# A Mamba layer stack on one core: the softplus correction moves from VectorE to GpSimd and ScalarE, and one product with C moves the other way

## The chip, the core and the metric

The kernel runs on one core of a Trainium2 chip. Its time is the device time of one launch in microseconds (us). Three runs of the kernel before took 16158.87, 16161.65 and 16184.59 us; their median is 16161.65 us.

## The reference

Sixteen sequences of 324 tokens (196 image patches and 128 text tokens) with 192 channels are embedded, normalized, and passed through sixteen Mamba layers; a mixture of sixteen experts follows. Nearly all of the time goes to the Mamba layers. For each layer, cut to what matters:

```python
h = rmsnorm(x, nw)
u, z = split(h @ in_w.T)                       # 2 x 384 channels
u = silu(causal_conv(u, cw, cb))               # 4 taps
dt_r, Bm, Cm = split(u @ xp_w.T)               # 48, 16, 16
dt = softplus(dt_r @ dtw.T + dtb)
A = -exp(a_log)
# scan over the 324 tokens, 384 channels x 16 states:
h = exp(dt * A) * h + (dt * u) * Bm
y = sum_n(h * Cm) + u * D
x = x + (y * silu(z)) @ ow.T
```

## The kernel before, in words

`run_layers` treats one layer of one sequence as a unit: 16 layers by 16 sequences are 256 units. Each engine runs its own endless program of steps, one step per unit, and the engines meet only at semaphores. A step `u` scans unit `u` and at the same time prepares the following ones: step-size work (softplus, z) for unit `p = u+1`, in-projection, convolution and x-projection for `k = u+2`, and the norm for `j = u+3`. The order of work on each engine is written out by hand: a step runs over `n = 0..15`, and each `n` holds one of sixteen scan passes and a few other pieces that are tied to that `n`.

One scan pass `s` covers 128 partitions by 972 elements (a quarter of the 16 states times 384 channels over 324 tokens). ScalarE writes `exp(dt*A)` into one of two PSUM buffers (`se_decay`, L602, three instructions), GpSimd writes `dtu*B` into one of four buffers (`ge_dbu`, L820), VectorE runs the scan into one of eight buffers `h` (`ve_scan`, L770). Then `h` is multiplied by C in place. VectorE does this from a PSUM copy of C that TensorE broadcasts once for four passes (`te_bcast` L439, `ve_product` L779). For the passes listed in `ON_POOL = (3, 7, 13)` GpSimd does it (`ge_product`, L828), from a copy `c_rep` in SBUF that a DMA has replicated. TensorE adds the products up, two passes at a time (`te_sum`, L452, eight matmul records). `SUM_AT` says at which `n` of the TensorE step each pair is added.

All small projections of TensorE share one PSUM bank `pj`, so they take strict turns with the ScalarE instruction that empties it: z in two halves (`te_z` L481, emptied by `se_z` L626), the output projection in two halves (`te_out` L496 and L498, emptied by `se_out` L632), u in two halves (`te_u` L516, `se_ur` L638), the convolution in two halves (`te_conv` L530, `se_conv` L645), the x-projection (`te_xp` L550), the step size in two halves (`te_dt` L559, emptied by `se_dt` L697/L698), and the sum of squares (`te_ss` L542).

The step size is `softplus(x) = relu(x) + log(1 + e)`, with `e = exp(-abs(x))`. The logarithm of a rounded `1 + e` loses digits of a small `e`, so the kernel corrects it. ScalarE computes `e` (`se_softplus` step 0, L704, at n = 0), `log(1 + e)` into `dtu` (step 1, L708, at n = 1), and the rounded `1 + e` into `u_pre` (step 2, L712, at n = 2, between the first z half and the decay of pass 3). VectorE then computes `(u_pre - 1) - dtu` into `dtu` in one instruction (`ve_log_error`, L794, after scan pass 3 and product 2). GpSimd builds `dt = dt + e` (L841, n = 4), `dt = dt - dtu` (L845, n = 8) and `dtu = dt * u` (L849, n = 8).

SyncE issues the DMAs in a fixed order, each behind the waits it needs. It stores `dt` and `dtu` to DRAM and loads them back replicated over partitions: four loads `dtu_rep` (`sp_load_dtu`, L914), each behind the GpSimd pass that last reads its buffer (12 to 15), and four loads `dt_rep` (`sp_load_dt`, L907), each behind the decay pass that last reads its buffer (12 to 15). All four `dtu_rep` loads and the last load of B stand ahead of the first `dt_rep` load. The next unit's decay pass 0 needs `dt_rep` 0.

Of the kernel before, what the change touches and what calls it, by code (L numbers as in the profile page):

```python
# [7 lines left out]
ALU = mybir.AluOpType  # L8
# [25 lines left out]
NR = 4  # L34
RING = 8
DRING = 4
ON_POOL = (3, 7, 13)
EPS = 1e-5
HALF_ULP = 2.0 ** -24

# [46 lines left out]
def embed(nc, cst, x_T, ins, raw_tables):  # L87
# [32 lines left out]
    with ExitStack() as ctx:  # L120
# [21 lines left out]
        with nc.Block() as block:  # L142
# [12 lines left out]
            @block.vector  # L155
            def _(dve):
                dve.memset(cst["eps"][:, :], EPS)
                dve.memset(cst["one"][:, :], 1.0)
                dve.memset(cst["ones96"][:, :], 1.0)
                dve.wait_ge(s_w, 32)  # L160
                done = 0
                for q in range(4):
                    hy, hx = q // 2, q % 2
                    oh, ow = (1 - hy), 2 * (1 - hx)
                    keep_h, keep_w = 1 - oh, 2 - ow
                    k_of = lambda a, b: w[:, 1 + a + b, 2 * q:2 * q + 2, :]
                    v = lambda i: wv[:, 2 * q:2 * q + 2, i, :]

                    for out, a, b in ((3, w[:, 0, 2 * q:2 * q + 2, :], k_of(keep_h, keep_w)),
                                      (1, v(3), k_of(keep_h, ow)),  # L170
                                      (2, v(3), k_of(oh, keep_w)),
                                      (0, v(1), k_of(oh, keep_w)),
                                      (0, v(0), k_of(oh, ow))):
                        wait(dve, s_v, done)
                        dve.tensor_tensor(v(out), a, b, ALU.add).then_inc(s_v, 1)
                        done += 1
# [129 lines left out]
def run_layers(nc, cst, x_T, params, weights, b_rows, dt_rows, dtu_rows):  # L306

    ident, ones96, sel_c, fold = cst["ident"], cst["ones96"], cst["sel_c"], cst["fold"]
    with ExitStack() as ctx:
# [74 lines left out]
        s_dtp = sem("s_dtp")  # L384
        s_dtev = sem("s_dtev")
        s_sp = sem("s_sp")
        s_d1 = sem("s_d1")
        s_dt = sem("s_dt")
        s_cq = sem("s_cq")
        s_z = sem("s_z")  # L390
# [170 lines left out]
            mm.then_inc(s_dtp, 1)  # L561


        SUM_AT = {3: 0, 6: 1, 7: 2, 10: 3, 11: 4, 13: 5}

        def tensor_step(pe, u, par, scan=True, a1=True, b1=True):

            p, k, j = u + 1, u + 2, u + 3
            for n in range(N):
                if scan and n % 4 == 1:  # L570
                    te_bcast(pe, u, par, n // 4)
                if n == 0:
                    te_ss(pe, j, b1)
                if n in (0, 1) and scan:
                    te_sum(pe, u, n - 2)
                if n in (1, 2) and b1:
                    te_z(pe, p, 1 - par, n - 1)
                if n in (3, 4) and scan:
                    te_out(pe, u, n - 3)
                if n in (5, 6) and a1:  # L580
                    te_u(pe, k, par, n - 5, scan, b1)
                if n in (8, 9) and a1:
                    te_conv(pe, k, n - 8)
                if n == 12 and a1:
                    te_xp(pe, k, par)
                if n in (13, 14) and a1:
                    te_dt(pe, k, n - 13)
                if scan and n in SUM_AT:
                    te_sum(pe, u, SUM_AT[n])
                if n == 7 and scan:  # L590
                    te_skip(pe, u, par, 0)
                    te_skip(pe, u, par, 1)
# [47 lines left out]
        def se_conv(act, k, half):  # L640
            reached(act, s_cv, 2 * k + half + 1)
            if half == 0:
                reached(act, s_ua, k)
                reached(act, s_d1, k)
            act.copy(half_of(u_pre, half), pj).then_inc(s_cvev, 1)  # L645

        def se_silu(act, k, par, b1):
# [43 lines left out]
        def se_dt(act, k, half):  # L691
            reached(act, s_dtp, 2 * k + half + 1)
            if half == 0:
                reached(act, s_sp, 3 * k)
                wait(act, s_dst[0], 16 * k)
                wait(act, s_dst[1], 16 * k)
            act.activation(half_of(exp_x, half), pj, ACT.Abs)  # L697
            act.activation(half_of(dt, half), pj, ACT.Relu).then_inc(s_dtev, 1)  # L698

        def se_softplus(act, p, step):  # L700
# [2 lines left out]
                reached(act, s_dtev, 2 * p + 2)  # L703
                act.activation(exp_x[:, :], exp_x[:, :], ACT.Exp, scale=-1.0).then_inc(s_sp, 1)  # L704
            elif step == 1:
                reached(act, s_sp, 3 * p + 1)
                wait(act, s_dst[1], 16 * p)
                act.activation(dtu[:, :], exp_x[:, :], ACT.Ln, bias=cst["one"][:, 0:1]).then_inc(s_sp, 1)  # L708
            else:
                reached(act, s_d1, p)  # L710
                reached(act, s_ua, p + 1)
                act.activation(u_pre[:, :], exp_x[:, :], ACT.Identity, bias=cst["one"][:, 0:1]).then_inc(s_sp, 1)  # L712

        def se_c_rows(act, p, par):
            reached(act, s_xpev, p + 1)
# [72 lines left out]
                              y_ps, z_act[par][:, :, :].rearrange("p i t -> p (i t)").rearrange("p (a b) -> p a b", a=2),  # L788
                              ALU.mult).then_inc(s_gate, 1)

        def ve_log_error(dve, p):

            reached(dve, s_sp, 3 * p + 3)
            dve.scalar_tensor_tensor(out=dtu[:, :], in0=u_pre[:, :], scalar=-1.0, in1=dtu[:, :],  # L794
                                     op0=ALU.add, op1=ALU.subtract).then_inc(s_d1, 1)

        def vector_step(dve, u, par, scan=True, a1=True, b1=True):
            p = u + 1
            other = 1 - par
            for n in range(N):  # L800
# [4 lines left out]
                if scan:  # L805
                    if n - 1 not in ON_POOL:
                        ve_product(dve, u, n - 1)
                if n == 3 and b1:
                    ve_log_error(dve, p)


        def ge_dbu(pool, u, s):
# [24 lines left out]
        def ge_dt(pool, p, par, step):  # L837

            if step == 0:
                reached(pool, s_sp, 3 * p + 1)  # L840
                pool.tensor_tensor(dt[:, :], dt[:, :], exp_x[:, :], ALU.add).then_inc(s_dt, 1)  # L841
            elif step == 1:
                reached(pool, s_dt, 3 * p + 1)
                reached(pool, s_d1, p + 1)
                pool.tensor_tensor(dt[:, :], dt[:, :], dtu[:, :], ALU.subtract).then_inc(s_dt, 1)  # L845
            else:
                reached(pool, s_dt, 3 * p + 2)
                reached(pool, s_ua, p + 1)
                pool.tensor_tensor(dtu[:, :], dt[:, :], u_act[par][:, :, :].rearrange("p i t -> p (i t)"), ALU.mult).then_inc(s_dt, 1)  # L849

        def gpsimd_step(pool, u, par, scan=True, a1=True, b1=True):
            p = u + 1
            for n in range(N):
                if scan:
                    ge_dbu(pool, u, n)
                    if (n - 4) % N in ON_POOL:
                        ge_product(pool, u if n >= 4 else u - 1, (n - 4) % N)
                if n == 4 and b1:
                    ge_dt(pool, p, 1 - par, 0)
                if n == 8 and b1:  # L860
                    ge_dt(pool, p, 1 - par, 1)
                    ge_dt(pool, p, 1 - par, 2)
                if n == 10:
                    ge_x_norm(pool, u + 3, 1 - par)

# [27 lines left out]

        def sp_store_dt(sp, p, which):

            reached(sp, s_dt, 3 * p + 2 + which)
            sp.sem_inc(s_go, 1)
            for s in (s_dur if which else s_dtr):
                wait(sp, s, 16 * p)
# [17 lines left out]
        def sync_step(sp, u, par, scan=True, a1=True, b1=True, reload=None):  # L917
# [9 lines left out]
                if reload and q < 2:  # L927
                    reload(q)
            if b1:
                for r in range(NR):  # L930
                    sp_load_dtu(sp, u, r)
                sp_load_b(sp, u, par, 3)
                for r in range(2):
                    sp_load_dt(sp, u, r)
            if reload:
                reload(2)
            if b1:
# [45 lines left out]
        with nc.Block() as block:  # L983
# [90 lines left out]

            @block.vector
            def _(dve):
                raise_counts(dve, s_scan, s_prod, s_gate, s_d1)
                for d in decay:
                    dve.memset(d, 0.0).then_inc(s_free, 1)
                for i in range(RING):  # L1080
# [670 lines left out]
def program(nc, ins, out):  # L1751
# [6 lines left out]
    with ExitStack() as ctx:  # L1758
        def sb(name, shape, dt=F32):
# [2 lines left out]
        cst = {  # L1762
            "ident": sb("ident", [128, 128]), "ones96": sb("ones96", [HC, HC]),
            "sel_c": sb("sel_c", [80, NQ, 128]), "fold": sb("fold", [128, 32]), "eps": sb("eps", [128, 1]),
            "one": sb("one", [128, 1]),
        }
        with ExitStack() as stream:
            x_T = stream.enter_context(nc.sbuf_tensor("x_T", [HC, 2, T], F32))
# [105 lines left out]
```

## Time and profile before

| what | us |
|---|---|
| median of three runs | 16161.65 |
| profiled execution, its own time | 16150.05 |
| its span in the trace | 16148.2 |
| VectorE busy | 13797.9 |
| TensorE busy (matmul) | 13519.5 |
| GpSimd busy | 13365.1 |
| ScalarE busy | 11298.1 |

The mean granted clock of TensorE over the span was 0.903.

The span is measured from the first to the last instruction; the own time is 1.85 us more. All rows below are from that one execution. A line number such as L770 is the line of the kernel file that issued an instruction; where no operand is named the row is about the queue itself. "Idle" in brackets is how long the engine sat idle ahead of a row and what it was released by. The granted clock (PEclk) is 1.00 where TensorE ran at 2.4 GHz and 0.50 where it ran at 1.2 GHz.

### The profile page before, as it was taken

The numbers are of one execution on the slowest core, as the hardware profiler recorded it, in microseconds if no ns is written. First come the engines' busy times: TensorE is split into PE (matmuls) and PEld (weight loads), VectorE is DVE, ScalarE is ACT, GpSimd is POOL, SyncE is SP. The second block draws the span as 40 slices with busy tenths as digits, with TensorE's granted clock in tenths as the row PEclk, the third lists the DMA queues.
The fourth block names the chain that finished last, engine by engine and source line by source line (L and its number), as shares of the span: only waits on it lengthen the run. The fifth ranks groups of instructions, "written<-read, shape, count | busy, mean of one in ns | idle before, by whom it ended". The sixth has DMA issues, their size and how long they took to land. (4 is left out here: it accounts for less than half of the span.)

```text
span 16148.2 us, 205785 instructions
## 1 busy us (share of the span) xinstructions
PE 13519.5 (84%) x52202; PEld 6684.0 (41%) x52202; DVE 13797.9 (85%) x9806; ACT 11298.1 (70%) x21632; POOL 13365.1 (83%) x6095
## 2 busy tenths in 40 slices
PE   6888888888888888888888888888888888887689
PEld 4334434433343343343434334444434433434367
DVE  2999999999999999999999999999999999993643
ACT  3777777777777777777777777777777777773111
POOL 1999999999999999999999999999999999990023
PEclk7989999999999999989999998888989999997799
DMA  2333333333333333333333333333333333331022
GB/s 71 114 118 110 112 122 108 115 112 120 108 116 119 112 111 118 114 110 124 108 115 111 121 109 113 118 114 111 109 123 108 115 115 117 110 119 32 9 52 58
DMA packets 714479, 1703.22 MB, mean 105 GB/s; under 512 B 89033, under 2 KB 369462, under 8 KB 714162
## 3 DMA queue, kind: packets, MB, share of 16 engines
q1 hardware_dynamic: 693666, 1685.54, 31.4%
q0 software_dynamic: 19968, 15.98, 0.6%
q14 instruction: 109, 0.89, 0.0%
q10 hardware_dynamic: 720, 0.55, 0.0%
q8 instruction: 16, 0.26, 0.0%
HBM read 1414.96 MB, written 286.74 MB: 105 GB/s over the span
## 5 line engine op out<-in xcount | busy, mean ns | idle before, releaser
L820 POOL TENSOR_TENSOR dbu<-dtu_rep,b_rep 128x972 f32<-128x972 f32 x4096 | 9131.1, 2250 | 1066.6 <-DVE h L770 1041.0
L770 DVE TENSOR_TENSOR_SCAN h<-ps,dbu 128x972 f32<-128x972 f32 x4096 | 8825.4, 2169 | 1050.6 <-ACT ps L602 1049.6
L602 ACT ACTIVATE ps<-dt_rep,A_cur 128x323 f32<-128x323 f32 x12288 | 5881.6, 521 | 987.0 <-DVE h L770 806.6
L452 PE MATMUL ps<-h,fold 128*32 128x486 f32 x16400 | 4149.9, 668 | 78.2 <-DVE h L779 77.1
L779 DVE TENSOR_TENSOR h<-h,ps 128x972 f32<-128x972 f32 x3329 | 3800.2, 1142 | 105.2 <-PE ps L439 102.4
L828 POOL TENSOR_TENSOR h<-h,c_rep 128x972 f32<-128x972 f32 x769 | 1964.0, 2554 | 2.2 <-DVE h L770 2.2
L452 PEld LDWEIGHTS ps<-h,fold 128*32 128x32 f32 x16400 | 854.7, 119 | 2453.0 <-issue 2002.0
L530 PE MATMUL ps<-u_raw,w_cv 128*128 128x162 f32 (+7 forms) x8256 | 1801.9, 371 | 2.8 <-ACT u_raw L638 1.5
L530 PEld LDWEIGHTS ps<-u_raw,w_cv 128*128 128x128 f32 x8256 | 1359.4, 190 | 458.4 <-ACT u_pre L645 115.7
L1632 POOL DMA_INDIRECT e_rows<-n_rows,e_ix x96 | 96.9, 1010 | 1306.0 <-issue 1213.8
L439 PE MATMUL ps<-c_rows,sel_c 16*128 16x324 f32 x2048 | 882.6, 512 | 332.6 <-DVE h L779 332.5
L516 PE MATMUL ps<-x_norm,w_u 96*128 96x324 f32 (+1 forms) x4128 | 987.4, 383 | 202.1 <-ACT u_raw L638 196.2
L481 PE MATMUL ps<-x_norm,w_z 96*128 96x324 f32 (+1 forms) x4112 | 1011.6, 390 | 168.9 <-ACT z_pre L626 168.2
L550 PE MATMUL ps<-u_act,w_x 128*128 128x324 f32 x1548 | 538.1, 488 | 575.1 <-ACT u_act L653 568.1
L498 PE MATMUL ps<-y_gated,w_o 128*96 128x324 f32 x3084 | 1008.4, 466 | 0.0
L481 PEld LDWEIGHTS ps<-x_norm,w_z 96*128 96x128 f32 x4112 | 677.6, 195 | 624.9 <-issue 273.5
L516 PEld LDWEIGHTS ps<-x_norm,w_u 96*128 96x128 f32 x4128 | 664.6, 190 | 517.6 <-ACT u_raw L638 259.8
L632 ACT COPY x_T<-ps 96x324 f32 (+1 forms) x514 | 218.2, 424 | 922.8 <-PE ps L498 922.8
L559 PE MATMUL ps<-xp_rows,w_dt 49*128 49x162 f32 (+1 forms) x2064 | 696.0, 467 | 169.3 <-ACT xp_rows L689 165.4
L645 ACT COPY u_pre<-ps 128x486 f32<-128x486 f32 x516 | 290.9, 564 | 673.9 <-PE ps L530 673.8
L439 PEld LDWEIGHTS ps<-c_rows,sel_c 16*128 16x128 f32 x2048 | 315.7, 192 | 1004.1 <-DVE h L779 834.1
L496 PE MATMUL ps<-x_T,ident 96*96 x1028 | 405.9, 476 | 388.0 <-ACT z_pre L626 386.2
(171 smaller groups left out, 14794.0 us busy)
## 6 DMA issues: line engine op xcount, KB each, us to landing
dtu_rep<-dtu_rows SPq DMA_DIRECT2D x1028, 486.0 KB, 4.0
dt_rep<-dt_rows SPq DMA_DIRECT2D x1028, 486.0 KB, 6.6
b_rep<-b_rows SPq DMA_DIRECT2D x1028, 162.0 KB, 2.6
dt_rows<-dt SPq DMA_DIRECT2D x257, 486.0 KB, 2.7
dtu_rows<-dtu SPq DMA_DIRECT2D x257, 486.0 KB, 2.7
c_rep<-b_rows SPq DMA_DIRECT2D x770, 162.0 KB, 6.0
w_cv<-in_w_cv SPq DMA_DIRECT2D x17, 768.0 KB, 8.0
b_rows<-xp_rows SPq DMA_DIRECT2D x258, 40.5 KB, 6.0
```

The source lines that it names most:

```text
L439: pe.matmul(c_ps, sel_c[64:80, q, :], c_rows[par][64:80, :], start=True, stop=True).then_inc(s_cbc, 1)
L452: mm = pe.matmul(y_ps[32 * r:32 * r + 32, half, :], fold[:, :], src[:, half * YW:(half + 1) * YW], start=(m in (0, 1)), stop=(m < 0))
L481: mm = pe.matmul(pj[:, lo:hi], w_z[:, c, it * 128:it * 128 + 128], x_norm[par][:, c, t:t + hi - lo], start=(c == 0), stop=(c == 1))
L498: mm = pe.matmul(pj[0:HC, 0:L], w_o[:, it, half * HC:(half + 1) * HC], y_gated[:, it, :], start=False, stop=(it == IT - 1))
L516: mm = pe.matmul(pj[:, lo:hi], w_u[:, c, it * 128:it * 128 + 128], x_norm[par][:, c, t:t + hi - lo], start=(c == 0), stop=(c == 1))
L530: mm = pe.matmul(pj[:, lo + skip:hi], w_cv[:, it * KC + KC - 1 - back, :], u_raw[:, it * L + t + skip - back:it * L + t + hi - lo - back], ...
L559: mm = pe.matmul(pj[:, lo:hi], w_dt[:, it * 128:it * 128 + 128], xp_rows[0:RB, t:t + hi - lo], start=True, stop=True)
L602: ins = act.activation(decay[s % 2][:, it * L + 1:(it + 1) * L], dt_rep[:, s % NR, it, 1:L], ACT.Exp, scale=A_cur[:, it * N + s:it * N + s ...
L770: dve.tensor_tensor_scan(h[s % RING][:, :, :].rearrange("p i t -> p (i t)"), decay[s % 2], dbu[s % DRING][:, :, :].rearrange("p i t -> p ( ...
L779: dve.tensor_tensor(h[s % RING][:, :, :], h[s % RING][:, :, :], c_ps.unsqueeze(1).broadcast_to([128, IT, L]), ALU.mult).then_inc(s_prod, 1)
L820: pool.tensor_tensor(dbu[s % DRING][:, :, :], dtu_rep[:, r, :, :], b_rep[:, q, :].unsqueeze(1).broadcast_to([128, IT, L]), ALU.mult).then_ ...
L828: pool.tensor_tensor(h[s % RING][:, :, :], h[s % RING][:, :, :], c_rep[:, at, :].unsqueeze(1).broadcast_to([128, IT, L]), ALU.mult).then_i ...
```

## The change

ON_POOL loses pass 3: GpSimd multiplies passes 7 and 13, VectorE the other fourteen, and one `c_rep` load per unit goes. The VectorE instruction `ve_log_error` goes. ScalarE gets a second pass at the same place (n = 2) that subtracts 1 from `u_pre` in place and waits for the first. GpSimd now subtracts `u_pre - 1` from `dt` and adds `dtu` to it in two instructions, so that it has four step-size instructions, at n = 3, 5, 7 and 8, where it had three. TensorE adds pair 1 at n = 5, between the two halves of u, where it did it at n = 6 behind both, and pair 3 at n = 11 just ahead of pair 4. SyncE issues two of the `dt_rep` loads between the `dtu_rep` loads.

```diff
-ON_POOL = (3, 7, 13)
+ON_POOL = (7, 13)
...
+                dve.memset(cst["minus_one"][:, :], -1.0)
...
-        SUM_AT = {3: 0, 6: 1, 7: 2, 10: 3, 11: 4, 13: 5}
+        SUM_AT = {3: (0,), 5: (1,), 7: (2,), 11: (3, 4), 13: (5,)}
...
-                if scan and n in SUM_AT:
-                    te_sum(pe, u, SUM_AT[n])
+                for m in SUM_AT.get(n, ()) if scan else ():
+                    te_sum(pe, u, m)
...
             else:
-                reached(act, s_d1, p)
+                reached(act, s_dt, 4 * p - 2)
                 reached(act, s_ua, p + 1)
                 act.activation(u_pre[:, :], exp_x[:, :], ACT.Identity, bias=cst["one"][:, 0:1]).then_inc(s_sp, 1)
+                reached(act, s_sp, 4 * p + 3)
+                act.activation(u_pre[:, :], u_pre[:, :], ACT.Identity, bias=cst["minus_one"][:, 0:1]).then_inc(s_sp, 1)
...
-        def ve_log_error(dve, p):
-
-            reached(dve, s_sp, 3 * p + 3)
-            dve.scalar_tensor_tensor(out=dtu[:, :], in0=u_pre[:, :], scalar=-1.0, in1=dtu[:, :],
-                                     op0=ALU.add, op1=ALU.subtract).then_inc(s_d1, 1)
...
-                if n == 3 and b1:
-                    ve_log_error(dve, p)
...
             elif step == 1:
-                reached(pool, s_dt, 3 * p + 1)
-                reached(pool, s_d1, p + 1)
-                pool.tensor_tensor(dt[:, :], dt[:, :], dtu[:, :], ALU.subtract).then_inc(s_dt, 1)
+                reached(pool, s_dt, 4 * p + 1)
+                reached(pool, s_sp, 4 * p + 4)
+                pool.tensor_tensor(dt[:, :], dt[:, :], u_pre[:, :], ALU.subtract).then_inc(s_dt, 1)
+            elif step == 2:
+                reached(pool, s_dt, 4 * p + 2)
+                pool.tensor_tensor(dt[:, :], dt[:, :], dtu[:, :], ALU.add).then_inc(s_dt, 1)
...
-                if n == 4 and b1:
-                    ge_dt(pool, p, 1 - par, 0)
-                if n == 8 and b1:
-                    ge_dt(pool, p, 1 - par, 1)
-                    ge_dt(pool, p, 1 - par, 2)
+                if n in (3, 5, 7, 8) and b1:
+                    ge_dt(pool, p, 1 - par, (3, 5, 7, 8).index(n))
...
-                for r in range(NR):
-                    sp_load_dtu(sp, u, r)
+                sp_load_dtu(sp, u, 0)
+                sp_load_dt(sp, u, 0)
+                sp_load_dtu(sp, u, 1)
+                sp_load_dtu(sp, u, 2)
+                sp_load_dt(sp, u, 1)
+                sp_load_dtu(sp, u, 3)
                 sp_load_b(sp, u, par, 3)
-                for r in range(2):
-                    sp_load_dt(sp, u, r)
```

## Rows read from the trace of the kernel before

**Rows 1.** List of waits: who waited for whom, total us, times, longest us.
```profile
DVE h L770 <- ACT ps L602: 1049.6, 876, 36.7
PE ps L496 <- ACT z_pre L626: 386.2, 256, 1.5
ACT ps L602 <- DMA dt_rep<-dt_rows: 149.9, 133, 2.9
```
**Rows 2.** Timeline of VectorE in one unit: start us, us, instruction, idle before.
```profile
6078.75 2.18 DVE L770 TENSOR_TENSOR_SCAN h<-ps,dbu 128x972 f32<-128x972 f32 x1 [1.46 <-ACT ps L602]
...
6082.98 2.17 DVE L770 TENSOR_TENSOR_SCAN h<-ps,dbu 128x972 f32<-128x972 f32 x1
...
6086.13 2.39 DVE L794 SCALAR_TENSOR_TENSOR dtu<-u_pre,dtu 128x972 f32<-128x972 f32 x1
6088.44 4.24 DVE L770 TENSOR_TENSOR_SCAN h<-ps,dbu 128x972 f32<-128x972 f32 x2
```
**Rows 3.** Timeline of ScalarE in the same unit.
```profile
6069.33 1.44 ACT L602 ACTIVATE ps<-dt_rep,A_cur 128x323 f32<-128x323 f32 x3 [0.53 <-DMA dt_rep<-dt_rows]
...
6079.55 1.10 ACT L712 ACTIVATE u_pre<-exp_x,one 128x972 f32<-128x972 f32 x1
6080.56 1.43 ACT L602 ACTIVATE ps<-dt_rep,A_cur 128x323 f32<-128x323 f32 x3
6081.92 0.56 ACT L626 COPY z_pre<-ps 128x486 f32<-128x486 f32 x1
```
**Rows 4.** Timeline of TensorE in the same unit.
```profile
6058.19 1.90 PE L550 MATMUL ps<-u_act,w_x 128*128 128x324 f32 x6 [2.20 <-ACT u_act L653]
...
6079.25 1.91 PE L481 MATMUL ps<-x_norm,w_z 96*128 96x162 f32 x8 [0.65 <-ACT z_pre L626]
6082.67 0.78 PE L496 MATMUL ps<-x_T,ident 96*96 x2 [1.51 <-ACT z_pre L626]
6083.28 1.80 PE L498 MATMUL ps<-y_gated,w_o 128*96 128x324 f32 x6
...
6092.63 1.91 PE L516 MATMUL ps<-x_norm,w_u 96*128 96x162 f32 x8 [0.79 <-ACT u_raw L638]
6094.47 1.83 PE L452 MATMUL ps<-h,fold 128*32 128x486 f32 x8
6096.95 1.82 PE L452 MATMUL ps<-h,fold 128*32 128x486 f32 x8 [0.65 <-DVE h L779]
```
**Rows 5.** Group of L452's matmuls: busy us, mean ns, idle before and releaser.
```profile
L452 PE MATMUL ps<-h,fold 128*32 128x486 f32 x16400 | 4149.9, 668 | 78.2 <-DVE h L779 77.1
```
**Rows 6.** Source view of L602: idle before it until, us, times.
```profile
  ACT A_cur L608: 7.9, 41
```
**Rows 7.** Short stretches: us; PE, PEld, DVE, ACT, POOL busy; PEclk, DMA share, GB/s.
```profile
6055.90:6057.40 1.50, 0.08 (x2) 0.00 (x0) 1.50 (x3) 1.49 (x4) 1.50 (x2) 1.00 0.43 91
...
6063.40:6064.90 1.50, 1.50 (x6) 0.38 (x4) 1.50 (x3) 1.50 (x4) 1.50 (x2) 0.50 0.93 299
```
**Rows 8.** Output projection to C broadcast in twelve successive units, the same columns.
```profile
5642.78:5649.28 6.50, 6.48 (x19) 2.64 (x20) 6.50 (x5) 3.41 (x8) 4.52 (x3) 0.74 0.03 7
...
5753.71:5760.21 6.50, 4.99 (x15) 2.03 (x16) 5.92 (x5) 3.51 (x9) 3.86 (x3) 0.74 0.00 0
...
6191.88:6198.38 6.50, 6.48 (x25) 2.85 (x25) 6.50 (x5) 3.48 (x8) 4.52 (x3) 1.00 0.04 4
```
**Rows 9.** Whole units (pass 2 to pass 2), and TensorE's timeline in the first.
```profile
5638.88:5695.18 56.30, 50.18 (x176) 23.35 (x177) 50.91 (x31) 42.16 (x81) 51.12 (x24) 0.82 0.34 114
...
6078.75:6133.26 54.51, 45.92 (x178) 21.48 (x178) 50.92 (x31) 42.41 (x82) 51.15 (x24) 0.94 0.34 113
...
5643.42 3.31 PE L498 MATMUL ps<-y_gated,w_o 128*96 128x324 f32 x6
```
**Rows 10.** Timelines of the SyncE queue and of GpSimd in the unit of rows 2.
```profile
6063.16 1.81 SPq L907 DMA_DIRECT2D dt_rep<-dt_rows  x3
...
6081.01 2.24 POOL L820 TENSOR_TENSOR dbu<-dtu_rep,b_rep 128x972 f32<-128x972 f32 x1 [1.20 <-DVE h L770]
```

More of the change, by code:

```diff
@@ L386, in run_layers @@
         s_sp = sem("s_sp")
-        s_d1 = sem("s_d1")
         s_dt = sem("s_dt")
@@ L643, in se_conv @@
                 reached(act, s_ua, k)
-                reached(act, s_d1, k)
+                reached(act, s_dt, 4 * k - 2)
             act.copy(half_of(u_pre, half), pj).then_inc(s_cvev, 1)
@@ L693, in se_dt @@
             if half == 0:
-                reached(act, s_sp, 3 * k)
+                reached(act, s_sp, 4 * k)
                 wait(act, s_dst[0], 16 * k)
@@ L705, in se_softplus @@
             elif step == 1:
-                reached(act, s_sp, 3 * p + 1)
+                reached(act, s_sp, 4 * p + 1)
                 wait(act, s_dst[1], 16 * p)
@@ L839, in ge_dt @@
             if step == 0:
-                reached(pool, s_sp, 3 * p + 1)
+                reached(pool, s_sp, 4 * p + 1)
                 pool.tensor_tensor(dt[:, :], dt[:, :], exp_x[:, :], ALU.add).then_inc(s_dt, 1)
             elif step == 1:
-                reached(pool, s_dt, 3 * p + 1)
-                reached(pool, s_d1, p + 1)
-                pool.tensor_tensor(dt[:, :], dt[:, :], dtu[:, :], ALU.subtract).then_inc(s_dt, 1)
+                reached(pool, s_dt, 4 * p + 1)
[4 more added lines that the diff above has]
+                pool.tensor_tensor(dt[:, :], dt[:, :], dtu[:, :], ALU.add).then_inc(s_dt, 1)
             else:
-                reached(pool, s_dt, 3 * p + 2)
+                reached(pool, s_dt, 4 * p + 3)
                 reached(pool, s_ua, p + 1)
@@ L894, in sp_store_dt @@
         def sp_store_dt(sp, p, which):
-            reached(sp, s_dt, 3 * p + 2 + which)
+            reached(sp, s_dt, 4 * p + 3 + which)
             sp.sem_inc(s_go, 1)
@@ L1076, in _ @@
             def _(dve):
-                raise_counts(dve, s_scan, s_prod, s_gate, s_d1)
+                raise_counts(dve, s_scan, s_prod, s_gate)
                 for d in decay:
@@ L1764, in program @@
             "sel_c": sb("sel_c", [80, NQ, 128]), "fold": sb("fold", [128, 32]), "eps": sb("eps", [128, 1]),
-            "one": sb("one", [128, 1]),
+            "one": sb("one", [128, 1]), "minus_one": sb("minus_one", [128, 1]),
         }
```

## The prediction

> **What bounds the kernel now.** I read the busy shares first: VectorE 85%, TensorE 84%, GpSimd 83%, so no engine is full and a loop of waits must set the time. The list of waits names the links: VectorE waits 1049.6 us for decay passes of ScalarE, 4.1 us in each of the 256 units; ScalarE waits for `dt_rep` loads; TensorE waits in every unit 1.51 us for the z copy before it may start the output projection [rows 1]. Then I followed one unit through the timelines, that which begins with scan pass 2 at 6078.75. I call times by their last digits from here.
>
> VectorE starts pass 2 at 78.75, having waited 1.46 for decay 2; every unit has this wait [rows 2]. So VectorE's queue starts afresh there, and two paths run from there to the sum of pair 2 (TensorE, 96.95), behind which the skip, the convolution, SiLU, the x-projection, the step size and the next unit's decays follow in turn:
>
> - The VectorE path: passes 2 to 6 with their products up to product 5. TensorE's sum 2 waited 0.65 for product 5 [rows 4].
> - The ScalarE and TensorE path: first z copy, the pass L712, decay 3, second z copy at 81.92 [rows 3], output projection from 82.67 in two halves, C broadcast, first half of u, a wait of 0.79 for the copy of u, second half, sum 1, sum 2 [rows 4].
>
> The second path has 0.79 + 0.65 = 1.44 us of slack in this unit. It does not always have it: the idle ahead of L452 until a product sums to 77.1 us [rows 5], 0.30 us per unit, so in many units the second path sets the time already.
>
> **The change part by part.** All numbers are us per unit, against the profiled execution's own 16150.05.
>
> *VectorE.* The correction leaves: its slot in the queue is 88.44 - 86.13 = 2.31 [rows 2]. Product 3 comes. From pass 3 to L794 it is 86.13 - 82.98 = 3.15, of which the pass holds 2.09 (two passes side by side end after 4.24), so a product holds 1.06 [rows 2]. Net -1.25 on the VectorE path.
>
> *ScalarE's second pass.* L712 holds its queue for 80.56 - 79.55 = 1.01 [rows 3]. The new pass has the same shape. It waits for its forerunner: the nearest case is a decay behind the copy of A that feeds it, 7.9 / 41 = 0.19 of idle [rows 6], and the 0.09 by which such passes overlap (1.10 long, 1.01 apart) is lost too. I take 1.01 + 0.19 + 0.09 = 1.29; the ends are 1.01 (no cost of the wait) and 1.6 (twice the wait and the overlap). Decay 3 and the second z copy stand behind it. Decay 3 ended at 80.56 + 1.43 = 81.99 and pass 3 started at 82.98, so about 1.0 is covered and VectorE waits some 0.35, which leaves its path 0.90 shorter. But the z copy has no cover: TensorE sat idle for it [rows 1, 4]. The second path gets +1.29, and the idle ahead of the output projection grows from 1.51 to 2.8.
>
> *TensorE's order.* Sum 1 (1.8 long, needs product 3, which ends near 89.7) now runs while ScalarE copies u, and the wait of 0.79 goes. The rows of other units have 0.73 to 0.79; I take -0.76 on the second path. Sums 3 and 4 ran back to back and still do: 0. The broadcast of C for passes 4 to 7 now waits for product 3; on the second path it is due behind two output halves and sum 0 (82.67 + 2.4 + 1.8 + 2.4 = 89.3, and 1.29 more), later than 89.7: 0.
>
> *Which path decides.* The VectorE path falls by 0.90, the second changes by 1.29 - 0.76 = +0.53. Where TensorE had waited for product 5, that slack (0.30 on average, rows 5) is used up first. So the path that remains is the second one, at +0.53 - 0.30 = +0.23. The relief of VectorE is worth nothing beyond that.
>
> *TensorE's clock.* In the unit read, TensorE is idle or nearly so around the x-projection (2.20 idle, [rows 4]; 0.08 busy of 1.50, [rows 7]), and some 5 us later the granted clock is 0.50, 1.2 GHz [rows 7]. After the shorter idle of 1.51 ahead of the output projection it stays at 1.00 in ten of twelve successive units and falls (0.74 over the stretch) in two [rows 8]. In such a unit the same output projection half takes 3.31 where it takes 1.80 [rows 4, 9], and the unit takes 56.30 against 54.51 [rows 9]. With the idle at 2.8, longer than the 2.20 that was followed by a fall, I take the clock to fall there in nearly every unit. A fall costs 1.51 by the row of L498 and up to 1.79 by the two units; 1.65 is between them. It now begins partly inside the idle, so I take 1.45 as its average cost, less what is paid already in 2 of 12 units (0.28): +1.17. The ends are 0 (no more falls than now) and +1.5 (a full fall everywhere).
>
> The Trainium skill speaks against this ("TensorE: Matmul & The Clock Gate", the closing section on why this matters for kernels): it asks only that no idle gap be longer than a length that the forecast gap of 2.8 does not reach. By that rule the clock would not fall, and the time would be that of the first rival. The trace does not agree with it, since it shows the fall behind a gap of 2.20.
>
> *Step-size loads.* The first `dt_rep` load went out at 63.16 [rows 10], behind the four `dtu_rep` loads, and decay 0 at 69.33 waited 0.53 for it [rows 3]. Scan 0 waits for decay 0 and decay 2 stands two places behind it in ScalarE's queue, so this wait is on both paths. The load may now go once decay 12 is done, near 55.2, eight us earlier. It should always have landed: -149.9 / 256 = -0.58. The ends are 0 (something else is as late, such as the sum of squares) and -0.58. The second `dt_rep` load now holds SyncE's queue until decay 13 (about 61.6), and the last `dtu_rep` load behind it goes out near 62.2, as late as now; nothing is lost. One `c_rep` load less only relieves the queue.
>
> *GpSimd.* Three products become two and three step-size passes become four: the same count of passes. A wait is added: the subtraction at n = 5 waits for ScalarE's new pass (until about 81.9). Behind it stands `dbu` 6, which waited for VectorE until 81.01 anyway [rows 10] and would end near 86.4, while pass 6 needs it after 92. The store of `dt` moves ahead. 0 on the path.
>
> *Sum.* 1.29 - 0.76 - 0.30 + 1.17 - 0.58 = +0.82 per unit, times 256 = +210, so 16360 for a profiled execution. That one lay 11.6 below the median of the runs shown, so I forecast 16372.
>
> **The rivals.**
>
> 1. *The clock does not fall after the longer idle.* Then the sum is -0.35 per unit, -90: 16072. For it: after 1.51 of idle the level mostly held. Against it: the fall behind 2.20, and the two units in twelve. This is the case that ends on the other side; it decides at the point at which the clock term is under 0.35, that is, at a fall in fewer than about four units of ten.
> 2. *VectorE's path sets every unit,* and TensorE's turn for the output projection is not what bounds. Then -0.90 - 0.58 = -1.48 per unit, -379: 15783. For it: VectorE is the busiest engine and sum 2 waited for product 5. Against it: 77.1 us in all for such waits, when a path that always sets the time would show 0.65 in each unit, 166.
> 3. *The clock falls in about half of the units,* clock term +0.5: +0.15 per unit, +38: 16200, or no change at all if it is a little rarer.
> 4. *The loads bring nothing and the fall is full:* 1.29 - 0.76 - 0.30 + 1.5 = +1.73, +443: 16605. For it: once everything is later by one us, a load that waits for decay 13 is later too, and the units in which the clock was low already can get a second low stretch. Against it: eight us of lead for the load that was waited for.
>
> **How the numbers follow.** My forecast (the clock falls in most units, loads help) has 0.62, with its own range of 16270 to 16470. Rival 1 has 0.19, rival 2 0.04, rival 3 0.10, rival 4 0.05. A measurement here can tell about 0.2%, 32 us, from no change. Rivals 1 and 2 are faster (0.23); rival 3 is split between same (0.05) and slower (0.05), and a forecast that comes out near its foot or a rival 1 near its top adds a little to same: 0.07. Slower gets 0.70. The range takes in the forecast's own and reaches down into rival 1: 16090 to 16480.
>
> **What would show it.** Right: the list of waits has PE L496 waiting near 2.8 a time for the z copy (L626); the `dt_rep` wait is gone; the wait of L516 for u_raw is nearly gone; PEclk over the output projection is near 0.75 in most units, and the mean granted clock drops below 0.903; VectorE waits longer for ScalarE and for the C broadcasts although its busy time falls by about 256 x 1.25 = 320 us. ScalarE's busy time rises by 284 us. Wrong: if PEclk over the output projection stays at 1.00, rival 1 holds; if sum 2 still waits for product 5, rival 2; if decays 0 still wait for a DMA, the load term is wrong; if the second z copy is late by much more or less than 1.29, the price of the new pass is.

## The result

| kernel | median us, four runs | profiled span | mean granted clock |
|---|---|---|---|
| before | 16168.92 | 16148.2 | 0.903 |
| changed | 16769.03 (16748.69 to 16805.88) | 16784.0 | 0.850 |

The changed kernel takes 1.0373 times as long (95% interval 1.035 to 1.0396): 600 us more, 2.34 us in each of the 256 units. The prediction had the sign, and +210.

The first views of the profile after are the list of waits, and the groups of instructions (busy us, mean ns, idle before and releaser). They answer to [rows 1, 5].

```profile
DVE h L772 <- ACT ps L602: 1737.5, 1678, 91.1
POOL dt L839 <- ACT u_pre L714: 895.1, 257, 6.9
PE ps L496 <- ACT z_pre L626: 677.3, 256, 2.7
```
```profile
L781 DVE TENSOR_TENSOR h<-h,ps 128x972 f32<-128x972 f32 x3585 | 4110.0, 1146 | 290.0 <-PE ps L439 279.2
L452 PE MATMUL ps<-h,fold 128*32 128x486 f32 x16400 | 4279.2, 678 | 0.0
L498 PE MATMUL ps<-y_gated,w_o 128*96 128x324 f32 x3084 | 1303.1, 575 | 0.0
```

TensorE waits 677.3 / 256 = 2.65 us for the z copy, where it waited 1.51. GpSimd's subtraction waits 3.5 us a time for the new pass, but no matmul and no scan waits for GpSimd. L452 never waits for a product any more: of the prediction's two paths up to sum 2, TensorE's is the one that decides. VectorE is less busy (13599.7 us, 198 less, where the prediction had 320) and waits more. No wait of a decay for `dt_rep` is left. A matmul of L498 takes 575 ns on average, where it took 466.

TensorE still waits for VectorE ahead of the C broadcasts, and less than before. The prediction had not looked at this wait; before and after:

```profile
PE ps L439 <- DVE h L779: 332.5, 381, 3.0
PE ps L439 <- DVE h L781: 183.6, 189, 2.0
```

ScalarE's timeline in one unit, to hold against [rows 3]:

```profile
6152.48 1.10 ACT L712 ACTIVATE u_pre<-exp_x,one 128x972 f32<-128x972 f32 x1
6153.62 1.10 ACT L714 ACTIVATE u_pre<-u_pre,minus_one 128x972 f32<-128x972 f32 x1
6154.63 1.42 ACT L602 ACTIVATE ps<-dt_rep,A_cur 128x323 f32<-128x323 f32 x3
6155.99 0.56 ACT L626 COPY z_pre<-ps 128x486 f32<-128x486 f32 x1
```

And TensorE's, to hold against [rows 4]:

```profile
6156.74 1.08 PE L496 MATMUL ps<-x_T,ident 96*96 x2 [2.65 <-ACT z_pre L626]
6157.62 3.23 PE L498 MATMUL ps<-y_gated,w_o 128*96 128x324 f32 x6
...
6167.47 1.82 PE L452 MATMUL ps<-h,fold 128*32 128x486 f32 x8
6169.23 1.91 PE L516 MATMUL ps<-x_norm,w_u 96*128 96x162 f32 x8
6171.06 1.83 PE L452 MATMUL ps<-h,fold 128*32 128x486 f32 x8
```

L712 to decay 3 is 2.15 us, where it was 1.01: the new pass holds the queue for 1.14. The first half of the output projection takes 3.23 where it took 1.80. The wait for the copy of u is gone, filled by sum 1 at 6167.47; sums 1 and 2 now stand apart and take 1.8 us each.

Six successive whole units (length; PE, PEld, DVE, ACT, POOL busy; PEclk, DMA share, GB/s), against [rows 9]:

```profile
5861.10:5921.98 60.88, 54.13 (x186) 25.38 (x185) 50.17 (x32) 43.35 (x82) 50.25 (x23) 0.81 0.31 102
5921.98:5980.19 58.21, 51.50 (x180) 23.85 (x180) 50.17 (x32) 43.35 (x82) 50.25 (x23) 0.82 0.32 108
5980.19:6038.89 58.70, 51.95 (x182) 24.32 (x180) 50.28 (x31) 43.35 (x82) 50.23 (x23) 0.83 0.31 103
6038.89:6093.53 54.64, 46.58 (x176) 22.26 (x175) 50.09 (x31) 43.36 (x82) 47.81 (x22) 0.91 0.33 110
6093.53:6151.68 58.15, 49.52 (x183) 23.06 (x181) 50.17 (x31) 43.46 (x83) 51.70 (x25) 0.88 0.31 103
6151.68:6209.27 57.59, 49.08 (x170) 22.52 (x170) 50.28 (x32) 43.24 (x82) 51.20 (x24) 0.84 0.32 104
```

VectorE and ScalarE are busy for the same time in each. The shortest unit, 54.64, has the highest clock, 0.91, and the longest, 60.88, the lowest, 0.81; between them the order is not strict. Over the output projection the clock is now below 1.00 in every one of twelve units looked at; two of them, against [rows 8]:

```profile
6044.09:6050.59 6.50, 6.35 (x18) 2.73 (x19) 5.89 (x4) 3.25 (x8) 6.50 (x4) 0.74 0.02 2
6098.73:6105.23 6.50, 5.76 (x12) 2.46 (x14) 6.39 (x4) 2.74 (x7) 6.50 (x4) 0.52 0.00 0
```

Counted over 220 successive units in the middle of each trace, the mean clock over the first half of the output projection is below 0.9 in 220 units here and in 47 before, and TensorE is at 1.2 GHz for 17.2 us of a unit where it was for 9.8. So the clock falls elsewhere in the unit too. Counts and times at 1.2 GHz below are taken in the same way.

### The profile page after: what moved, and what is told of

The parts are those of the page before. It is cut to its first block and busy times, and to the rows that moved or that the text cites. A ratio compares the mean times of both kernels' runs of the same rounds, so it can differ in the third digit from the quotient of the medians.

```text
span 16784.0 us, 205153 instructions
## 1 busy us (share of the span) xinstructions
PE 14390.6 (86%) x52202; PEld 7023.7 (42%) x52202; DVE 13599.7 (81%) x9806; ACT 11553.5 (69%) x21889; POOL 13129.5 (78%) x6096
## 5 line engine op out<-in xcount | busy, mean ns | idle before, releaser
L602 ACT ACTIVATE ps<-dt_rep,A_cur 128x323 f32<-128x323 f32 x12288 | 5878.1, 521 | 254.5 <-DVE h L772 202.8
L781 DVE TENSOR_TENSOR h<-h,ps 128x972 f32<-128x972 f32 x3585 | 4110.0, 1146 | 290.0 <-PE ps L439 279.2
L452 PE MATMUL ps<-h,fold 128*32 128x486 f32 x16400 | 4279.2, 678 | 0.0
L452 PEld LDWEIGHTS ps<-h,fold 128*32 128x32 f32 x16400 | 859.5, 121 | 2384.1 <-issue 2358.1
L498 PE MATMUL ps<-y_gated,w_o 128*96 128x324 f32 x3084 | 1303.1, 575 | 0.0
L839 POOL TENSOR_TENSOR dt<-dt,u_pre 128x972 f32<-128x972 f32 x257 | 574.2, 2234 | 895.1 <-ACT u_pre L714 895.1
L550 PE MATMUL ps<-u_act,w_x 128*128 128x324 f32 x1548 | 709.9, 614 | 591.3 <-ACT u_act L653 584.3
L822 POOL TENSOR_TENSOR h<-h,c_rep 128x972 f32<-128x972 f32 x513 | 1150.6, 2243 | 5.5 <-DVE h L772 5.5
L439 PE MATMUL ps<-c_rows,sel_c 16*128 16x324 f32 x2048 | 960.7, 553 | 183.6 <-DVE h L781 183.6
L496 PE MATMUL ps<-x_T,ident 96*96 x1028 | 474.2, 548 | 679.2 <-ACT z_pre L626 677.3
L498 PEld LDWEIGHTS ps<-y_gated,w_o 128*96 128x96 f32 x3084 | 664.7, 216 | 522.4 <-issue 322.6
L559 PE MATMUL ps<-xp_rows,w_dt 49*128 49x162 f32 (+1 forms) x2064 | 835.3, 544 | 48.4 <-ACT xp_rows L689 46.0
```

The lines of the kernel that those rows point to most:

```text
L439: pe.matmul(c_ps, sel_c[64:80, q, :], c_rows[par][64:80, :], start=True, stop=True).then_inc(s_cbc, 1)
L452: mm = pe.matmul(y_ps[32 * r:32 * r + 32, half, :], fold[:, :], src[:, half * YW:(half + 1) * YW], start=(m in (0, 1)), stop=(m < 0))
L498: mm = pe.matmul(pj[0:HC, 0:L], w_o[:, it, half * HC:(half + 1) * HC], y_gated[:, it, :], start=False, stop=(it == IT - 1))
L559: mm = pe.matmul(pj[:, lo:hi], w_dt[:, it * 128:it * 128 + 128], xp_rows[0:RB, t:t + hi - lo], start=True, stop=True)
L602: ins = act.activation(decay[s % 2][:, it * L + 1:(it + 1) * L], dt_rep[:, s % NR, it, 1:L], ACT.Exp, scale=A_cur[:, it * N + s:it * N + s ...
L781: dve.tensor_tensor(h[s % RING][:, :, :], h[s % RING][:, :, :], c_ps.unsqueeze(1).broadcast_to([128, IT, L]), ALU.mult).then_inc(s_prod, 1)
```

## The experiments

Each ratio is to the kernel before on the same chip. All times are medians of four runs. The experiments ran on four chips, on which the kernel before took 16113 to 16177 us, so a difference between experiments is taken from their ratios, times 16169 us.

**1. The second pass behind the second z copy** (in the changed kernel).
```diff
                 if n in (2, 3) and b1:
                     se_z(act, p, n - 2)
+                if n == 3 and b1:
+                    se_softplus(act, p, 3)      # the minus_one pass alone
```


> The changed kernel with one move: ScalarE's new second pass (u_pre - 1) stands behind the second z copy instead of ahead of decay 3. Theory A (the late z copy widens TensorE's idle ahead of the output projection, and the clock falls there): the idle of L496 goes back to about 1.5 us a time, the mean granted clock back to 0.90 or more, and the time to 15900 to 16100, since the filled u wait and the earlier dt_rep load are left as gains. Rival B (the extra instructions on ScalarE cost what they cost wherever they stand in the first half of the step, because VectorE waits for decays): 16500 to 16770. Rival C (the order of the SyncE loads or the new order of the sums is what costs): unchanged near 16770.

Measured: 16031.34 us, ratio 0.9913 (0.9896 to 0.9929), clock 0.881. The wait of L496 is 386.1 us in all, 1.51 a time. Moving one ScalarE instruction by some 2 us gives back 744 us. B falls, and C as the whole cause: the pass costs by where it stands. The clock stayed below the 0.90 that A had named: over the output projection it is low in 109 of 220 units, where the kernel before, with the same idle, has 47.

**2. The load order alone** (in the kernel before; the SyncE part of the diff).

> The kernel before with the new order of the dt_rep and dtu_rep loads alone. Theory A: no wait of decay 0 for a DMA is left, 0.58 us per unit less, 16020. Rival C: the new load order costs by itself, 16400 or more. If the sum of squares or TensorE is as late as the load was, no change.

Measured: 16006.04 us, ratio 0.9897 (0.9881 to 0.9914), some 167 us or 0.65 per unit. The term stood at 0.58. No decay waits for a DMA any more. The clock rose too, to 0.917 from 0.90, with 7.5 us of a unit at 1.2 GHz instead of 9.8, so the closeness of the two numbers is in part luck.

**3. The idle filled** (in the changed kernel). TensorE computes one piece of the second z half twice.
```diff
-            for it, lo, hi, t in pieces(half):
+            for it, lo, hi, t in (pieces(1)[1:] if half else []) + pieces(half):
```


> The changed kernel; TensorE computes the last piece of the second z half twice (the same values into the same place), 1.1 us of matmuls that end before ScalarE comes to copy. The second z copy is exactly as late as in the changed kernel, only TensorE's idle ahead of the output projection is 1.5 instead of 2.65. Theory A, clock: the granted clock over the output projection goes back to 1.00 in most units, and the time falls to 16150 to 16350. Rival B, lateness by itself: no change, 16770, or slower.

Measured: 15989.49 us, ratio 0.9891 (0.9874 to 0.9908), clock 0.907: below the kernel before. TensorE in one unit:

```profile
5724.47 3.00 PE L481 MATMUL ps<-x_norm,w_z 96*128 96x324 f32 x12 [0.65 <-ACT z_pre L626]
5729.02 0.78 PE L496 MATMUL ps<-x_T,ident 96*96 x2 [1.56 <-ACT z_pre L626]
5729.64 1.80 PE L498 MATMUL ps<-y_gated,w_o 128*96 128x324 f32 x6
```

From the start of the z half to the output projection it is 4.55 us here and 4.56 in the changed kernel: the z copy is as late. Only the idle is shorter, 1.56, and L498 takes 1.80 again in this unit. Over the output projection the clock is low in 75 of 220 units, where it was in all. More work on TensorE took 780 us away, where A had 420 to 620. Lateness alone (rival B) could not have done that. It is 3.0 us per unit, more than one fall costs by any row (1.5 to 1.8): TensorE is at 1.2 GHz for 9.1 us of a unit where it was for 17.2, so falls elsewhere in the unit went too.

**4. Both passes behind the second z copy** (`se_softplus(act, p, 2)` at n == 3).

> The changed kernel with both passes on u_pre behind the second z copy. The copy may start once TensorE has finished the half, about 0.6 us earlier than in the kernel before; idle of L496 about 0.9. Theory A: at or below the first kernel of this set, 15800 to 16050, with the mean clock above 0.90. Rival B: 16500 or more, since ScalarE has the same work ahead of decay 4.

Measured: 16002.02 us, ratio 0.9892 (0.9875 to 0.9908), clock 0.897. TensorE waits only 0.79 a time for the z copy (202.1 us in all), and nothing is gained over experiment 1 beyond 29 us. Time and idle are near what stood for A, the clock is just under its 0.90. What the earlier copy gave may have gone into another wait, which was not tested: sums now wait for the products of GpSimd, whose subtraction waits for the late passes. In the changed kernel no matmul had this wait.

```profile
PE ps L452 <- POOL h L822: 819.3, 512, 1.8
```

**5. One pass more in the kernel before.**
```diff
+                reached(act, s_cv, 2 * p + 2)
+                act.activation(u_raw[:, :], exp_x[:, :], ACT.Identity, bias=cst["one"][:, 0:1])
                 act.activation(u_pre[:, :], exp_x[:, :], ACT.Identity, bias=cst["one"][:, 0:1]).then_inc(s_sp, 1)
```


> The kernel before with one ScalarE instruction more: the pass of L712 runs twice at its place (once into u_raw, which is free there), so that decay 3 and the second z copy are about 1.0 us late and nothing else changes. Theory A, clock: TensorE's idle ahead of the output projection grows from 1.5 to 2.5 us, the granted clock falls over it in most units, and the time rises by 300 us or more, to 16450 to 16900, with a mean clock near 0.86. Rival B, lateness alone, at 1.0 less the slack of 0.3 per unit: 16330 to 16370 with the mean clock at 0.90.

Measured: 16223.82 us, ratio 1.0067 (1.0049 to 1.0085), clock 0.869. A miss of both. The clock fell as A said, over the output projection in all of twelve units (PEclk 0.74 to 0.79), but lateness and fall together cost 0.4 us per unit, not 1.2 or more. So the late z copy and its fall of the clock do not by themselves explain 600 us. The waits show where part of the cost may have gone. The loads are no longer waited for: 12.4 us of such waits are left of [rows 1]'s 149.9, 0.54 per unit. And TensorE, itself later, waits less for VectorE's products, 123.0 us ahead of the C broadcasts for 332.5 and 1.9 ahead of the sums for 77.1, together 1.11 per unit. Of this slack ahead of TensorE's matmuls the prediction had counted only the 77.1 us.

**6. The old order of the sums** (in the changed kernel; `SUM_AT` with 6: 1, 10: 3, 11: 4).

> The changed kernel with pair 1 added at n = 6 again, behind both halves of u, and pair 3 at n = 10. If the wait for the copy of u is on the path as the prediction had it (0.76 us per unit), the time is 0.76 x 256 = 195 us more, 16960. If the new order of the sums was part of what made it slow, it falls, to 16600 or less. If the path runs elsewhere, no change.

Measured: 16380.9 us, ratio 1.0165 (1.0148 to 1.0182): 336 us, 1.31 per unit, less, where the prediction's term said 0.76 more. The wait for the copy of u is back (187.6 us in all). TensorE in one unit:

```profile
6006.68 1.91 PE L516 MATMUL ps<-x_norm,w_u 96*128 96x162 f32 x8 [0.73 <-ACT u_raw L638]
6008.51 2.06 PE L452 MATMUL ps<-h,fold 128*32 128x486 f32 x16
6010.50 1.91 PE L468 MATMUL ps<-u_act,w_d 128*128 128x324 f32 x8
```

Sixteen records, both sums, take 2.06 us; eight take 1.83 in the changed kernel. A sum writes two of four groups of 32 output rows (`y_ps[32 * r:32 * r + 32]`, r = s % 4), and its neighbour the other two. That this is why they overlap was not tested: no run puts two sums into the same groups. The clock changed as well, 14.6 us of a unit at 1.2 GHz instead of 17.2, so the 1.31 is not the price of the order alone.

**7. Does adjacency matter?** The kernel of experiment 6 with the skip product between sums 1 and 2 (`if n == 6 and scan: te_skip(...)`): the same work in another order.

> The changed kernel with the old order of the sums, and the skip product (L468) moved between sum 1 and sum 2, so that the two no longer stand back to back; TensorE's work is the same. Theory D: two sums back to back overlap on TensorE, since they write different 32-row groups (2.06 us for both in the old-order kernel, 1.83 for one alone), and splitting them is what the changed order lost: the time rises from 16381 by about 1.5 us per unit, to 16650 to 16800. Rival E: what the old order brought back came from where the clock falls, or from the unfilled wait for the copy of u: then moving the skip changes nothing, 16340 to 16420.

Measured: 16622.52 us, ratio 1.0298 (1.0281 to 1.0316), 215 us or 0.84 per unit slower than experiment 6, although its clock is higher (0.888 against 0.866). The time is 30 us under D's range and far from E's.

```profile
6004.42 1.82 PE L452 MATMUL ps<-h,fold 128*32 128x486 f32 x8
6006.17 1.91 PE L468 MATMUL ps<-u_act,w_d 128*128 128x324 f32 x8
6008.01 1.82 PE L452 MATMUL ps<-h,fold 128*32 128x486 f32 x8
```

In the changed kernel the sums are as far apart and the wait for the copy of u is filled, and still it is 121 us slower than this one, with a clock of 0.850. Filling that wait gave nothing that the clock did not take back.

**8. The new order of the sums in the kernel before.**

> The kernel before with the new order of the sums alone. The prediction's term: 0.76 us per unit less where TensorE's path decides, nothing where product 5 does, 16000 to 16130. Theory D (adjacent sums overlap, splitting them costs 1.6 us less the 0.76 of wait that is filled): in units where product 5 decides, no change; in the others 0.8 more: 16180 to 16350.

Measured: 16259.06 us, ratio 1.0051 (1.0034 to 1.0068): slower there too, by 0.3 us per unit, in D's range. The clock hardly differs (0.894, and 0.898 for the kernel before on that chip). TensorE waits more for product 5 here: 206.5 us ahead of L452, where it was 77.1.

**9. The old load order in the changed kernel.**

> The changed kernel with the old order of the dt_rep loads. The prediction's own term says 0.58 us per unit slower, 16917. The theory now: in the longer unit of the changed kernel the loads land in time in either order (the kernel before with one pass more had 12 us of such waits in all), so no change within 40 us of 16769.

Measured: 16747.52 us, ratio 1.0382 (1.0364 to 1.0399), the changed kernel's own being 1.0373. No decay waits for a DMA in either order. The load term is nothing in the longer unit.

**10. Old sums, second pass late** (experiments 1 and 6 together).

> The changed kernel with the old order of the sums and the second pass behind the second z copy. If the 212 us that are left after the sums are undone come from the late z copy (its lateness and the clock behind it), this is at or below the kernel with the second pass alone moved, 15900 to 16040. If they come from product 3 on VectorE or the GpSimd order, it stays near 16380.

Measured: 15954.89 us, ratio 0.9865 (0.9849 to 0.9882). With this the two causes make a table (ratio to the kernel before, all other parts as in the changed kernel):

| | second pass ahead of the z copy | behind it |
|---|---|---|
| new order of the sums | 1.0373 | 0.9913 |
| old order | 1.0165 | 0.9865 |

Both undone, the product on VectorE, the four GpSimd passes and the loads are 1.35% faster than before; the loads alone gave 1.03% in experiment 2. Each cause costs more where the other is: the early pass 744 us with the new order and 485 with the old, the new order 336 us with the early pass and 78 with the late one.

**11. More fills.** In the changed kernel, with the doubled z piece, six identity matmuls ahead of the x-projection (`te_fill`), and the old sums with the doubled z piece alone:

> The changed kernel with the doubled z piece and six more matmuls of the identity ahead of the x-projection (1.3 us at full clock, in an idle of 2.2 us that waits for SiLU). Theory A: the fall over the x-projection, the step size and the sums behind it goes too; with 1.5 us per fall on the path the time is 15650 to 15850, and the mean clock above 0.95. If the falls there are not on the path, as with the doubled z piece alone: 15990. If the fill itself delays the x-projection: above 16000.

> The doubled z piece with the old order of the sums. As for the version before it: 15990 if the unit keeps its 54.61 us, down to 15800 if the shorter path shows, 16150 by rival E.

Measured: 16811.04 (ratio 1.0424, 1.0406 to 1.0443) and 16214.34 (1.0047, 1.0031 to 1.0064). Two misses. The first is above 16000, which stood for a fill that delays the x-projection, but the x-projection only waits less ahead of its start, 0.75 us for SiLU where it waited 2.28. With both idles filled the mean clock is 0.904 and the time 0.5%, 82 us, worse than without any fill. TensorE in one unit:

```profile
6043.82 1.44 PE L439 MATMUL ps<-c_rows,sel_c 16*128 16x324 f32 x2 [3.08 <-DVE h L788]
6045.20 3.46 PE L452 MATMUL ps<-h,fold 128*32 128x486 f32 x8
6048.58 2.40 PE L481 MATMUL ps<-x_norm,w_z 96*128 96x324 f32 x8
6051.64 3.00 PE L481 MATMUL ps<-x_norm,w_z 96*128 96x324 f32 x12 [0.65 <-ACT z_pre L633]
6056.19 1.17 PE L496 MATMUL ps<-x_T,ident 96*96 x2 [1.55 <-ACT z_pre L633]
6057.16 3.14 PE L498 MATMUL ps<-y_gated,w_o 128*96 128x324 f32 x6
```

The fall over the x-projection is gone, in all 220 units. Instead TensorE waits 3.08 for VectorE ahead of a C broadcast, a wait of 0.68 on average in experiment 3. The clock is low behind it, over the broadcast, a sum and the first z half. The doubled z half runs at full clock, 3.00 as in experiment 3. And the clock is low again over the output projection, in all 220 units, behind the same idle of 1.55 that was followed by a fall in 75 in experiment 3. So the length of the idle just ahead does not by itself decide whether the clock falls. The same fill that took 780 us away in experiment 3 takes 191 away with the old sums, and leaves the fall in 155 of 220 units. A fill can move the fall instead of removing it.

**12. Both passes late, with the identity matmuls, and with the old sums.**

> The changed kernel with both passes on u_pre behind the second z copy, and the six identity matmuls ahead of the x-projection. Theory A: the early z copy (0.6 us) now pays because no fall takes it back: at or below the kernel with both idles filled, 15550 to 15800. If the clock is not what holds that version, it stays at 16002.

> Both passes on u_pre behind the second z copy, and the old order of the sums. Theory D with the clock theory: a path 0.8 us or more shorter than with the new order of sums; if every unit stays at the 54.61 us that the version with the new sums shows, nothing comes of it, 16002; if it leaves that length, 15800 to 15950. Rival E: 16002 or slower by the unfilled wait, 16100.

Measured: 15959.38 (ratio 0.99, 0.9884 to 0.9917) and 15965.14 (0.989, 0.9874 to 0.9907). Neither leaves the place that experiment 4 has (0.9892). The second kernel's TensorE:

```profile
5772.90 1.40 PE L542 MATMUL ps<-sq,ones 96*96 96x324 f32 x4 [1.13 <-ACT dt L698]
5775.97 3.46 PE L452 MATMUL ps<-h,fold 128*32 128x486 f32 x8 [1.68 <-POOL h L822]
```

and two of its units:

```profile
5969.75:6024.30 54.55, 45.14 (x179) 21.71 (x178) 49.72 (x32) 43.33 (x83) 50.00 (x24) 0.91 0.32 110
6024.30:6078.90 54.60, 45.16 (x179) 21.68 (x178) 49.78 (x32) 43.36 (x83) 50.05 (x24) 0.91 0.32 110
```

All 220 units counted have this length within 0.1 us. The low clock lies behind the idle of 1.68, a wait for GpSimd's product, ahead of the first sum of a step, and that sum takes 3.46.

**13. The sum of squares twice** (in that kernel), to fill this idle, and the same with the identity matmuls.
```diff
-            for c in range(2):
+            for c in (0, 1, 0, 1):
                 mm = pe.matmul(pj[0:HC, 0:L], ones96[:, :], sq[:, c, :], start=(c == 0), stop=(c == 1))
```


> The kernel with both passes late and the old sums, and the sum of squares computed twice (1.2 us of matmuls more in the 1.7 us in which TensorE waits for a product). If the low clock at the end of the unit holds its length at 54.61, it goes and the unit gets shorter: 15700 to 15900, mean clock above 0.93. If not, 15965 or, where the second sum of squares is itself late, 16000 to 16200.

> The same with six identity matmuls ahead of the x-projection. Clock theory: as the version with the sum of squares twice or better, 15650 to 15900. If a fill only moves the fall elsewhere, 15965 or more.

Measured: 15639.89 us, ratio 0.9672 (0.9656 to 0.9689), clock 0.918; and 15765.52 (0.9742, 0.9726 to 0.9758). The first is the fastest kernel here, 528 us under the kernel before, a little better than forecast, though its clock stayed under the 0.93. The second is inside its range but slower than the first: there the identity matmuls cost. In one unit of the first:

```profile
5633.37 3.81 PE L542 MATMUL ps<-sq,ones 96*96 96x324 f32 x8 [1.13 <-ACT dt L698]
5637.12 2.07 PE L452 MATMUL ps<-h,fold 128*32 128x486 f32 x8
```

The sum takes 2.07. But eight matmuls of the sum of squares take 3.81 where four took 1.40, so in this unit the low clock lies over the doubled group itself; it does so in 176 of 220 units. What went is low time as a whole, 7.5 us of a unit at 1.2 GHz for 10.2, and waits for GpSimd ahead of the sums, 319.1 us in all for 820.8. Which of the two shortened the unit was not tested. Units of 51.63 to 53.76 us appear between some of 56:

```profile
5482.49:5534.12 51.63, 43.51 (x182) 21.96 (x181) 49.60 (x31) 43.39 (x82) 48.93 (x24) 0.97 0.35 121
5534.12:5590.28 56.16, 49.78 (x181) 24.48 (x180) 50.26 (x31) 43.45 (x82) 54.20 (x26) 0.82 0.32 108
```

## Why the prediction was right in sign and wrong in size

- *The path.* Right: TensorE's turn for the output projection, behind ScalarE's z copy, decides, and VectorE's relief is worth nothing beyond its slack. Rival 2 is out. The slack was too small: it counted the waits ahead of the sums (77.1 us) and not those ahead of the C broadcasts, which went from 332.5 to 183.6 us, 0.58 per unit.
- *The second pass.* Right: 1.14 where 1.29 stood, and idle of 2.65 where 2.8 stood.
- *TensorE's order.* **This step failed.** It said that sum 1 "now runs while ScalarE copies u, and the wait of 0.79 goes", for -0.76. The wait went, but sums 1 and 2, which overlapped, were split: 2 x 1.83 - 2.06 = 1.60 us more of TensorE. The term is +0.84 by these rows. Measured, with the clock that came with it, it is +1.31 in the changed kernel (experiment 6) and +0.3 in the kernel before (experiment 8). Experiment 7, the same work with the two sums parted, shows that the adjacency counts: 0.84. The prediction had priced a sum by a row where it stood alone: in [rows 4] sum 2 waits 0.65 for product 5 and starts after sum 1 has ended.
- *Loads.* **This step failed too.** Right for the kernel before (0.65 for 0.58), wrong for the changed kernel, where the old order costs nothing (experiment 9): a longer unit has no such wait to remove. The end 0 of that term was the right one.
- *TensorE's clock.* Right that it falls over the output projection, in 220 units of 220. Rival 1 is out. The rule of the Trainium skill that the prediction cited ("TensorE: Matmul & The Clock Gate", the closing section) did not hold here: the clock fell behind a gap of 2.65 in every unit counted. Experiment 3 shows that the time goes with TensorE's idle and clock and not with the lateness of the z copy. But the idle just ahead is not the whole condition. At 1.50 to 1.56 of idle the clock is low over the output projection in none of 220 units (experiments 2 and 10), in 47 (before), 75 (experiment 3), 109 (experiment 1) or 220 (both idles filled). The size cannot be read as one term: it depends on what else stands on the path, from 0.4 us per unit for lateness and fall together (experiment 5) to 780 / 256 = 3.0 for the low clock that experiment 3 takes away.

With the two wrong terms replaced (+1.60 and +0.58) and the pass at 1.14, the sum reads 0.82 + 1.60 + 0.58 - 0.15 = 2.85 against a measured 2.34, and 2.27 with the slack of 0.58 ahead of the C broadcasts. That is a check on the sign and order of the terms, not on each, and that it closes so well is luck: the clock term in it is still the forecast 1.17, which no run measured by itself.

What stays open: why the same fill is worth 780 us with the new sums and 191 with the old, and what besides the idle just ahead decides whether the clock falls. In the units listed for the changed kernel the falls lie at other places from one unit to the next; how the length of a unit and the place of the falls settle on each other was not tested by itself.

## What to carry to other kernels

Before an instruction is moved into a TensorE wait, look at whether its neighbours overlapped: read the time of the pair, not of one. A wait that TensorE can afford in the path's arithmetic may still cost through the clock; price it from a unit of the same trace in which the clock fell. Redundant matmuls that end before the wait does can take the fall away, as in experiment 3, or bring it back elsewhere, as in experiment 11: measure the whole unit, not the place of the fill. A gain that removes a wait is worth only what of that wait is left once the other parts of the change have moved it.

## What the hardware showed that was not expected

Two sums into different groups of 32 output rows took 2.06 us back to back and 1.83 us each alone. Redundant matmuls made the kernel faster: 1.1 us more of them per unit took the changed kernel from a ratio of 1.0373 to 0.9891, and a second sum of squares took another version from 0.9890 to 0.9672; six identity matmuls added to the first made it slower again, 1.0424. In four versions (experiments 4, 10 and both of 12) all 220 units counted are 54.61 us long within 0.1 us, with different orders of work on TensorE and idles of 0.79 or 1.50 ahead of the output projection. In the slowest version, with both idles filled, all are 58.03. The two changes of experiment 12, forecast to shorten such a unit, left its length as it was.
